# Where an adapter's intermediate product, its difference and its loads stand in eight passes of a fused convolution and matmul kernel

## What is computed

```python
y   = conv1d(x, weight, 9 taps, padding 4, 4 groups) + cond @ c_weight.T + bias    # x: (32, 128, 2048)
# in 8 groups b of 4 samples, each row 2048 long:
Ax  = y @ (mixed lora_A[b]).T        # rank 32, and the same with the shared lora_A
out = x + y @ W + ffn_bias + Ax @ (mixed lora_B[b]).T + Ax_shared @ lora_B_shared.T   # W: 2048 x 2048
```

## Time and profile before

| | |
|---|---|
| median of 3 runs | 1736.31 us (1734.83 to 1737.27) |
| the profiled execution | 1739.94 us, its span 1737.7 us |
| TensorE busy | 1666.7 us (96%) |
| VectorE busy | 1216.4 us (70%) |
| ScalarE busy | 735.8 us (42%) |
| mean granted TensorE clock | 0.983 |
| DMA, mean over the span | 250 GB/s |

### The profile page before, as it was taken

The page is one execution under the profiler, slowest core; times in us unless marked ns, Lnnn a source line. Parts: engine busy times, 40 slices in busy tenths (PEclk is TensorE's granted clock), DMA queues, the critical chain, the costliest instruction groups (busy, mean ns, idle before and its releaser), DMA issues.

```text
span 1737.7 us, 22370 instructions
## 1 busy us (share of the span) xinstructions
PE 1666.7 (96%) x8240; PEld 1415.9 (81%) x8240; DVE 1216.4 (70%) x1777; ACT 735.8 (42%) x978; POOL 154.6 (9%) x200
## 2 busy tenths in 40 slices
PE   9999999999999999999999999977878899999999
PEld 6799999887888899988888888866656688887887
DVE  7888888955544799999965444657557644557776
ACT  6776777633223666655623122432333311123221
POOL 0010010224200000000001340000000000000100
PEclk9999999999999999999999999999998899999999
DMA  8978777888857678777777986866767699899885
GB/s 248 282 242 289 260 250 251 295 292 288 297 196 243 200 248 273 265 234 268 256 216 262 332 300 217 248 166 183 202 162 192 207 314 327 306 314 273 225 227 164
DMA packets 192772, 434.97 MB, mean 250 GB/s; under 512 B 51956, under 2 KB 91476, under 8 KB 188024
## 3 DMA queue, kind: packets, MB, share of 16 engines
q1 hardware_dynamic: 170664, 353.69, 60.8%
q0 software_dynamic: 20992, 75.51, 16.4%
q10 hardware_dynamic: 1008, 4.34, 0.9%
HBM read 279.05 MB, written 154.42 MB: 249 GB/s over the span
## 4 chain that ended last, share of the span: by engine, by line
PE 81%; DVE 8%; DMA 7%; issue 2%; ACT 1%; SPq 0%; DVEq 0%; ACTq 0%
PE acc L2266 48%; PE cps L2131 14%; PE cps L2338 5%; PE acc L2338 4%; DMA axs_d<-axd_hl 4%; PE cps L2181 3%; PE acc L2098 2%; PE acc L2165 2%; DVE g L1564 2%; DMA a_raw<-mixed_A 1%; DMA b_raw<-mixed_B 1%; DVE y_t L1492 1%; PE acc L2215 1%; PE acc L2371 1%; DVE w_lo L1480 1%
## 5 line engine op out<-in xcount | busy, mean ns | idle before, releaser
L2266 PE MATMUL acc<-w_hi,y_t 128*128 128x512 f32 x2560 | 712.1, 392 | 3.4 <-issue 1.9
L2266 PEld LDWEIGHTS acc<-w_hi,y_t 128*128 128x128 f32 x2560 | 475.6, 189 | 99.8 <-issue 3.5
L2266 PE MATMUL acc<-w_lo,y_t 128*128 128x512 f32 x1280 | 396.2, 391 | 0.0
L2266 PEld LDWEIGHTS acc<-w_lo,y_t 128*128 128x128 f32 x1280 | 241.1, 188 | 51.7
L1115 ACT COPY x_q<-x_raw 32x512 f32<-32x512 f32 x248 | 269.6, 1087 | 20.8 <-DVE x_lo L1581 13.4
L2131 PE MATMUL cps<-cw,x_hi 128*128 128x256 f32 (+2 forms) x1088 | 243.9, 312 | 0.4 <-DVE x_lo L1774 0.4
L2131 PE MATMUL cps<-cw,x_lo 128*128 128x384 f32 (+2 forms) x768 | 180.9, 283 | 0.0
L2131 PEld LDWEIGHTS cps<-cw,x_hi 128*128 128x128 f32 x1088 | 176.4, 189 | 3.6 <-DVE x_lo L1774 1.2
L2338 PE MATMUL cps<-w_hi,y_t 128*128 128x512 f32 x348 | 121.2, 409 | 31.9 <-DVE y_t L1492 31.9
L1574 DVE COPY x_q<-x_raw 32x512 f32<-32x512 f32 x248 | 147.9, 596 | 4.4
L1160 ACT CAST y_t<-g 128x1024 fp32r<-128x1024 f32 x63 | 66.4, 1053 | 194.1 <-PE acc L2266 158.3
(11 more groups left out here) (243 smaller groups left out, 2213.9 us busy)
## 6 DMA issues: line engine op xcount, KB each, us to landing
g<-U SPq DMA_DIRECT2D x80, 512.0 KB, 7.6
A<-g SPq DMA_DIRECT2D x64, 512.0 KB, 4.3
g<-A SPq DMA_DIRECT2D x64, 512.0 KB, 5.5
x_raw<-in_x SPq DMA_DIRECT2D x31, 1024.0 KB, 4.9
U<-g SPq DMA_DIRECT2D x48, 512.0 KB, 5.1
g<-in_L_ffn_kernel POOLq DMA_DIRECT2D x32, 512.0 KB, 6.2
T<-g POOLq DMA_DIRECT2D x32, 512.0 KB, 4.7
g<-in_x SPq DMA_DIRECT2D x32, 512.0 KB, 6.1
```

The lines of the kernel that those rows point to most:

```text
L2266: ins = T.matmul(acc[:, b, m, :], y_buf[b][:, c, part, :], wt[:, w, m * 512:(m + 1) * 512], start=(c == 0 and part == 0 and wt is w_hi), s ...
```

## The change

Six things are changed, in phase 4 but for one:

1. The difference of the second pair moves back: on ScalarE behind `a_split` and two `hi_part`, on VectorE to behind U3, and on SyncE its store, now by itself, behind the first quarter's store.
2. The load of lora_A moves from behind the second pair's stores to the front of the pass's loads.
3. Ax of the second pair goes to the bank of L22 (`acc[:, 1, 1]`). It no longer waits for `ax_both` of the first pair, but for the addition of L22 of the pass before (`bank_out`), in pass 0 for VectorE's last evacuation of phase 3. The waits for `ax_both` stand ahead of the products that write the banks.
4. In the last pass four first loads of phase 5 are issued: lora_B, the x rows, U3 and U2 of the first pair.
5. In the last pass ScalarE splits three weight tiles ahead of the second pair's difference.
6. GpSimd's first `combine` also waits for the fourth `pre_add` of phase 1.

```diff
-        ax_ps = [cps[:, 2, 0:2 * P]] + [acc[:, 0, 1, j * 2 * P:(j + 1) * 2 * P] for j in range(2)]
+        ax_ps = [cps[:, 2, 0:2 * P]] + [acc[:, j, 1, 0:2 * P] for j in range(2)]
@@ SyncE
                 sp.dma_start(axs_2[p], ax_words[:, j]).then_inc(axs_out[j], 16)
+            def store_two_axd(q, j):
+                p = 2 * q + j
                 sp.wait_ge(axd_lo_ready, p + 1)
                 sp.dma_start(axs_d[p], axd_words).then_inc(axd_out, 16)
+            def load_u2(u):
+                p, b = u % NP, u % 2
+                if p >= 2:
+                    sp.wait_ge(u4_out[b], 16 * (p // 2))
+                else:
+                    sp.wait_ge(stage_out[1], 16 * 2 * NP + 32 * (QS - 1 + p))
+                sp.dma_start(u2_buf[b], U2_d[p]).then_inc(u2_in[b], 16)
@@ (in the steps of phase 5 the first pair's load_xres, load_stage, load_b and U2 load fall away)
                 if more:
+                    load_a(first_pair(r + 1))
                     for j in range(2):
                         load_pass_y(r + 1, j)
                     load_b(first_pair(r + 1))
                 else:
                     for j in range(2):
                         load_y(5 * NP + j)
+                    load_b(5 * NP)
...
                 else:
                     load_t(5, 4)
                     load_t(5, 5)
+                    load_xres(5 * NP)
                 store_two_ax(r, 0)
+                store_two_axd(r, 0)
                 if more:
                     load_two_ax(r + 1, 0)
                 else:
                     load_t(5, 6)
+                    load_stage(5 * NP)
+                    load_u2(5 * NP)
                 store_two_ax(r, 1)
+                store_pass(r, 0)
+                if not more:
+                    load_t(5, 7)
+                store_two_axd(r, 1)
                 if more:
-                    load_a(first_pair(r + 1))
                     load_two_ax(r + 1, 1)
-                store_pass(r, 0)
-            load_t(5, 7)
@@ GpSimd
             pool.wait_ge(x_lo_ready, 2 * (NP - 1))
+            pool.wait_ge(pre_added, 4)
@@ ScalarE
                 ax_hi(u + 1)
+                if not last:
+                    a_split(u + 2)
+                    for e in range(1, 3):
+                        hi_part(r + 1, e)
+                else:
+                    for c in range(3, 6):
+                        split_t(5, c)
                 axd_hi(u + 1)
                 if not last:
-                    a_split(u + 2)
-                    for e in range(1, 4):
-                        hi_part(r + 1, e)
-            for c in range(3, 6):
-                split_t(5, c)
+                    hi_part(r + 1, 3)
@@ VectorE
                 ax_lo(u + 1)
-                axd_lo(u + 1)
                 if not last:
                     a_split(u + 2)
...
                 pass_u3(r)
                 if last:
                     split_t(5, 5)
+                axd_lo(u + 1)
+                if last:
                     y_lo(5 * NP)
@@ TensorE, pass_ax_part
-                if j == 0 and r >= 1:
-                    pe.wait_ge(pass_u, 2 * r)
-                pe.wait_ge(ax_both, a)
+                if j == 1:
+                    bank_out(r, ADD_L22)
+                    if r == 0:
+                        pe.wait_ge(evac_dve, evac_no(4 * NP - 1) + 1)
@@ TensorE, one_pass
+                if r == 0:
+                    pe.wait_ge(ax_both, 3 * NP)
                 pass_product(r, 3, EV_P6)
...
                 if F == 4:
-                    pe.wait_ge(ax_both, 3 * NP + 2 * r + 2)
+                    pe.wait_ge(ax_both, 3 * NP + 2 * r + 1)
                 pass_product(r, 5, EV_P7)
...
+                if F == 4:
+                    pe.wait_ge(ax_both, 3 * NP + 2 * r + 2)
                 pass_lora(r, 1, 1, EV_L22, alone=True)
```

More of the change, by code:

```diff
@@ L799, in step @@
                     load_stage(u)
-                if f in LORA_PHASES:
+                if f in LORA_PHASES and u != 5 * NP:
                     load_xres(u)
@@ L816, in step @@
                     sp.dma_start(ax_words[:, u % 2], axs_2[p]).then_inc(axs_in[u % 2], 16)
[L817 to L822, removed]
+                if f == 5 and p >= 1:
+                    load_u2(u)
                 if f < 1:
```

## The result

| | before | after |
|---|---|---|
| median | 1736.79 us (1734.83 to 1739.66) | **1661.62 us** (1660.60 to 1662.35) |
| the profiled execution, its span | 1739.94 us, 1737.7 us | 1660.60 us, 1658.8 us |
| mean granted TensorE clock | 0.983 | 0.999 |

What follows compares the result with a forecast made beforehand. The prediction took a loop of VectorE waits in phase 4, with no engine full, as the bound. Its terms, 50.5 + 6.3 + 6.6 - 1 + 8.4 - 2 = 69 us, took 1736.3 us to 1667 us, range 1656 to 1692.

Steps and rivals of the forecast that it cites:

- The mechanism: Phase 4: VectorE stands 6.2 us for the first difference's store and 4.0 us for lora_A, in a 31.6 us loop.
- The length of a pass: Phase 4: without the waits TensorE's own 23.05 us bounds a pass, taken as 23.3 us.
- The six lengths: Phase 4, six passes, second product to second product: 190.3 us falls to 139.8, a gain of 50.5 us.
- The wait before the first of the six passes: Phase 4, TensorE's wait before the second product at 1143.01 goes: 6.3 us gained.
- DMA lateness, -2 us: Phase 4, passes 2 to 5, each with a weight load: late transfers take back 2 us.
- Loop (a): Phase 4, transfers as a whole: 22.1 us of DMA busy time in 23.3 us, a share of 0.95.
- The rival that transfers close the loop: Phase 4: passes of 24.3 to 26.5 us, 6 to 19 us back, 1673 to 1686 us; chance 0.25.
- The store as the next bound: Phase 4, first difference's store: loop of 11.4 us plus landing, 22.4 at 11.0 us; decides at 12.
- The last pass: Phase 4, second product to phase 5: 30.2 us falls to 23.6, 6.6 us gained, some 3 us idle left.
- The 1 us for the clock: Slow clock behind the stop left at the start of phase 5: 1 us off the last pass's gain.
- the bound of +4.5: Start of phase 1, GpSimd's work moved away: up to 4.5 us gain if its loads caused TensorE's loss; 0 taken.
- The lower end of the range: Whole kernel: 1656 us, given as the sum with 23.05 us passes, no late transfers and GpSimd's later start's gain.

Runs made afterwards that it cites:

- Experiment 1: Kernel before with only lora_A's load moved to the front of the pass's loads: 1710.08 us, ratio 0.9843.
- experiment 2: Kernel after without the other bank, the four first loads of phase 5 and GpSimd's later start: 1674.77 us, ratio 0.9641.
- experiment 6: Kernel after with spare DRAM copies ahead of the first difference's store in passes 1 to 6: 1661.17 us with 512 KB, 1666.85 us with 1 MB.
- experiment 7: Kernel after, last pass's splits of weight tiles 4 and 5 behind L21's addition: 1658.45 us; the last difference's low part too: 1657.44 us.
- experiment 5: Kernel after with phase 5's four first loads back in phase 5's first step: 1667.09 us, ratio 0.9590.
- experiment 4: Kernel after with GpSimd's combine starting where it was, without the wait for the fourth pre_add: 1666.01 us, ratio 0.9590.

## Why the prediction was right, and where it was off

- **The mechanism** was right: two waits of VectorE in one loop, for the store of the first difference and for lora_A's load behind it. Experiment 1 takes out one, experiment 2 both, and the second carries 62 of the 75 us.
- **The length of a pass.** Taken as 23.3 us, measured 23.01. TensorE's own length, 23.05 us from phase 6's spacing plus two Ax, was the number, and the 0.25 us added for "a few tenths more than phase 6's spacing" were not there in passes 2 to 6. The six lengths that the sum counts are 138.7 us where 139.8 were forecast: 1.1 of the missed us.
- **The wait before the first of the six passes**: 6.3 forecast, 6.4 measured.
- **DMA lateness, -2 us: nothing.** Loop (a) forecast a share of 0.95, and 0.88 to 0.96 were measured, so the share was right. What was wrong is that such a share delays anybody: with 512 KB more a pass stood at 0.97 to 1.00 and the time did not move. The rival that transfers close the loop, given 1673 to 1686 us, fell with it.
- **The store as the next bound.** The landing was expected at 8.0 to 11.0 us, "just covered", deciding at 12. It is 8.8 to 10.3 us in passes 1 to 5, 7.6 in pass 6 and 12.0 in pass 0, where VectorE comes to it later and doesn't wait. VectorE waits 0.9 and 0.8 us in two passes, which TensorE covers. The loop is the right one. What it had too small is SyncE's part, 0.2 us for 0.2 to 1.1, so by the estimate of experiment 6 it decides from 10.9 to 11.8 us on: the next bound is about one us away.
- **The last pass**: 6.6 less 1 us forecast, 7.0 measured. The stop of "some 3 us" at the start of phase 5 is there with 2.86, for the reason given. The 1 us for the clock does not show in this stretch, as it falls behind the stop: there the granted clock is 0.65 from 1293.1 to 1298.0 us and 1.6 us are lost (experiment 7). It depends on the execution: of the eight profiled executions with a stop of 2.3 to 3.4 us at this place five lose these 1.6 us and three lose nothing.
- **Part 3**: nothing forecast, nothing measured, in both kernels.
- **Part 4**: 8.4 us forecast and 8.5 us between the two profiled executions, but the experiment that undoes it gives 4.2 to 5.5. The 2.9 us for the slow matmuls are in the traces: from this adapter matmul to the next it is 14.51 us before, 14.43 when the wait is back and 11.80 after. The wait is what was sized from a single execution: 5.57 us is near the top of the five, whose mean is 4.5 (experiment 5). That the two profiled executions agree with the forecast to 0.1 us is luck, as the 1.6 us of the last point are in their difference too.
- **Part 6 is the step that failed.** Taken as zero "as the wait there ends on VectorE", it is worth 4.4 us, the bound of +4.5 that the prediction itself had. Ending on VectorE was read as having nothing to do with GpSimd. But VectorE was late because its splits took longer beside GpSimd's subtractions, 4.42 instead of 2.36 us for two (experiment 4). The place of GpSimd's work afterwards was safe, though its end was forecast 13 us late ("near 541"): the work took 88 us there instead of 95.6, and its last memset runs at 527.82, 29 us before the convolution takes the buffer back at 556.83:

```profile
439.72 0.54 POOL L1014 DMA_DIRECT2D x_q<-T  x1 [81.70 <-DVE g L1709]
...
527.82 0.13 POOL L1034 MEMSET x_q<- 128x16 f32 x1
```

- **Two figures of the prediction don't follow from their terms.** The lower end of the range, 1656 us, is said to be the sum with 23.05 us, no late transfers and part 6's gain; these give 1659. And 128 KB take 0.4 to 0.7 us at the rates of the earlier trace rows, not "under 0.5 us at any rate"; nothing hung on it.

The sum, term by term, between the two profiled executions: 78.9 us went where the terms gave 68.8. Of the 10.1 us more, 5.4 are the start up to phase 4 (part 6, with what differs between executions), 3.1 the six passes (2 of them the DMA term, 1.1 the pass length), 1.4 the last pass, of which 1 is the clock's term, and 0.1 each the first wait and phases 5 and 6. By the medians it is 75.2 us, 3.7 less than by these two executions, of which the one before (1739.94 us) is slower than all four of the table and the one after the fastest of its four. So the median came out within 6 us of the forecast, with part 6 missing from the sum and part 4 somewhat too large in it.

The rule that one ring's descriptors are consumed in order (the Trainium skill, DMA: Bandwidth & Descriptors, Queues, rings and completion order) was weighed as a reason against the change. The row that it was weighed with holds here as well, a landing of 8.8 to 10.3 us for 128 KB behind the `pass_out` loads, where the page's sum for one transfer (Anatomy of one DMA) gave an estimate of 2.3. That section takes its sum from transfers that GpSimd issues, and this store goes out on SyncE's queue. How much stands ahead matters less than the rule alone suggests: 512 KB and 1 MB more directly ahead of the store delayed its landing by 0.7 and 1.5 us in the mean.

## What to carry to other kernels

When no engine is full in a stage, look for the loop: the waits of one engine in a row, and what its next instruction releases. Price each wait with the loop's own period, check that a full engine takes over (here the same work in another phase gave its length to 0.2%), and expect nothing from letting a third engine run ahead. A wait that ends on a compute engine is not explained until the lengths of that engine's instructions have been set beside those of the same instructions elsewhere: an engine that neither waits for the others nor is waited for can still slow one of them. And an instruction that is free of urgency should stand behind the ones that are awaited, above all if it waits for a transfer itself.

## What the runs showed of the hardware

- Two-input instructions of VectorE and GpSimd that ran at the same time both took longer: two splits of a 128x1024 tile on VectorE 4.42 instead of 2.36 us, a 128x512 subtraction on GpSimd 2.15 instead of 1.29 us. It was so in all five profiled executions in which they met at that place, and in none of the other seven.
- The DMA engines stood at a share of 0.97 to 1.00 in six passes in a row with 512 KB more (263 to 287 GB/s), and the time did not change. The share alone is no sign of a bound.
- The landing of a 128 KB store in a busy queue depends little on what is put ahead of it: 9.5, 10.2 and 11.0 us in the mean with 0, 512 and 1024 KB more, about 1.5 us for a MB, while the DMA engines' share for a MB was 3.5 to 3.7 us.
- TensorE's granted clock was 1.00 in every window of phase 4 once its stops were gone; before, it was 0.95 in a pass with 6.5 us of idle time and 0.80 in the last pass. The clock gave back some 2.3 us a pass (25.3 less 23.05 us), a quarter of what the six passes gained.
- A stop of 2.86 us before the same product was followed by a granted clock of 0.65 over 4.9 us in one execution and of 1.00 in another (the kernel after and that of experiment 5).
